# Packed expert weights, one column read per tile, three weight loads per group and 48 matmuls at three starts, in a two-layer attention and expert kernel

## The reference, cut to what matters

```python
x = x + L0_attention(layernorm(x), ctx)             # 16 heads, rotary
x = x + L0_ffn(layernorm(x), gate_w, w13, w2)       # 64 experts, 8 per token, inner width 128
x = x + L1_attention(layernorm(x), ctx)             # over the 256 features: softmax(q^T k) v
x = x + L1_ffn(layernorm(x), router_w, ...)         # 16 experts, 4 per token, inner width 224
```

## Time and profile before

| | us |
|---|---|
| median of 3 runs | 764.34 (762.84 to 764.79) |
| the profiled execution | 764.58 |
| its span, first to last instruction | 762.8 |
| PE busy | 506.1 (66%) |
| PE weight loads | 377.7 (50%) |
| DVE busy | 378.6 (50%) |
| ACT busy | 224.9 (29%) |
| GpSimd (POOL) busy | 351.0 (46%) |
| DMA | 162.57 MB, mean 213 GB/s |

### The profile page before, as it was taken

One profiled execution on the slowest core, in us unless ns is written; L12 is line 12 of the kernel. 1 busy time (PEld: TensorE's weight loads), 2 busy tenths in 40 slices (PEclk: granted clock), 3 DMA queues, 4 the chain that ended last, 5 costly groups with the idle time before them and its releaser, 6 DMA issues.

```text
span 762.8 us, 12322 instructions
## 1 busy us (share of the span) xinstructions
PE 506.1 (66%) x3519; PEld 377.7 (50%) x3519; DVE 378.6 (50%) x1235; ACT 224.9 (29%) x578; POOL 351.0 (46%) x476
## 2 busy tenths in 40 slices
PE   1725986878867323998879951677618878777760
PEld 1611543434432113977668840555517767666750
DVE  8955555877773530443334425888522222222226
ACT  0550353555555101332223311344302111211210
POOL 9483111445544550554455460144465545455530
PEclk9975888998996655999999975677859999999995
DMA  5199997644665796799974328611247767787837
GB/s 166 45 191 309 310 279 212 176 153 135 204 206 184 256 416 191 235 341 323 302 263 165 92 93 306 270 56 63 78 145 227 247 225 252 227 249 248 282 128 275
DMA packets 88291, 162.57 MB, mean 213 GB/s; under 512 B 13742, under 2 KB 58814, under 8 KB 86448
## 3 DMA queue, kind: packets, MB, share of 16 engines
q1 hardware_dynamic: 62208, 104.83, 43.1%
q0 software_dynamic: 13968, 32.29, 11.6%
q10 hardware_dynamic: 12064, 24.84, 11.1%
HBM read 103.56 MB, written 66.78 MB: 223 GB/s over the span
## 4 chain that ended last, share of the span: by engine, by line
PE 17%; DMA 14%; issue 12%; SPq 8%; DVE 5%; POOL 1%; another core or an unknown queue 1%; POOLq 1%; ACT 1%; DVEq 1%
DMA hd_side<-held 5%; PE hd_ps_up L1216 5%; DMA listed<-sc_empty,sc_index 2%; DMA sc_tile_rows<-listed 2%; PE hd_ps_out L1222 2%; DMA rows<-hd_side_out,hd_side_target 2%; SPq L426 2%; SPq L424 2%; DMA sc_rows<-rows 2%; PE sc_ps L1697 2%; PE hd_ps_x L1194 1%; PE sc_ps L1759 1%; SPq L1604 1%; PE sc_ps L1709 1%
## 5 line engine op out<-in xcount | busy, mean ns | idle before, releaser
L990 DVE TENSOR_REDUCE at_top<-at_ps_top 128x2 f32<-128x512 f32 x128 | 83.3, 683 | 59.6 <-PE at_ps_top L901 54.3
L1363 POOL DMA_INDIRECT rows<-hd_out,hd_rows x64 | 62.4, 975 | 72.9 <-DVE hd_out L1314 45.9
L1062 ACT ACTIVATE at_prob<-at_ps_score 128x512 f32<-128x512 f32 x128 | 72.3, 594 | 53.7 <-PE at_ps_score L919 42.4
L1759 PEld LDWEIGHTS sc_ps<-sc_t_turned,e_up_w 128*112 128x112 f32 x672 | 82.2, 183 | 5.7 <-issue 3.0
L1216 PE MATMUL hd_ps_up<-hd_x_turned,e_arena 128*128 128x160 f32 x512 | 84.9, 310 | 0.0
L1759 PE MATMUL sc_ps<-sc_t_turned,e_up_w 128*112 128x128 f32 x672 | 83.6, 279 | 1.9 <-DMA e_down_w<-in_down 1.8
L1216 PEld LDWEIGHTS hd_ps_up<-hd_x_turned,e_arena 128*128 128x128 f32 x512 | 78.3, 197 | 8.9 <-issue 6.2
L685 POOL DMA_INDIRECT held<-e_extended,e_address x64 | 63.1, 986 | 33.7 <-issue 18.9
L901 PE MATMUL at_ps_top<-e_arena 96*128 96x256 bf16 x256 | 58.0, 316 | 25.2 <-PEq L107 21.3
L1660 POOL DMA_INDIRECT rows<-sc_out,sc_target x42 | 41.3, 982 | 67.9 <-DVE sc_out L1903 61.7
L1351 DVE TENSOR_TENSOR hd_inner<-hd_silu,hd_ps_up 128x160 f32<-128x160 f32 x64 | 20.6, 321 | 92.1 <-ACT hd_silu L1301 62.0
(11 more groups left out here) (266 smaller groups left out, 930.5 us busy)
## 6 DMA issues: line engine op xcount, KB each, us to landing
e_arena<-in_weights SPq DMA_DIRECT2D x52, 384.0 KB
e_up_w<-in_up SPq DMA_DIRECT2D x42, 448.0 KB
held<-e_empty ACTq DMA_DIRECT2D x16, 960.0 KB, 5.7
hd_rows<-held SPq DMA_DIRECT2D x15, 768.0 KB
e_down_w<-in_down SPq DMA_DIRECT2D x42, 224.0 KB
sc_rows<-rows SPq DMA_DIRECT2D x8, 1024.0 KB, 13.7
sc_tile_rows<-listed SPq DMA_DIRECT2D x42, 144.0 KB
parts<-op_parts SPq DMA_DIRECT2D x8, 576.0 KB
```

The costliest lines, as they stand in the source:

```text
L990: nc.vector.reduce_max(top[:, 2 * h:2 * h + 2], ps_top[at % TOPS][:], AX_X).then_inc(top_found, 1)
L1062: nc.scalar.activation(prob[at % RING][:], ps_score[at % SCORES][:], ACT.Exp, scale=scale).then_inc(prob_ready, 1)
L1363: nc.gpsimd.indirect_dma_start(rows_out, to, out_ap, None, bounds_check=TOKENS * LAYER0.chosen - 1, oob_is_err=False).then_inc(semaphore, 16)
L1759: op = nc.tensor.matmul(ps_up[u % 2][:, part, c * P:(c + 1) * P], up_w[u][:, k, at:at + W], t_turned[u % 2][:, k, :], start=k == 0, stop=k ...
```

## The change

- The second experts' up and down weights become one array in DRAM, per expert 128 rows of 896 + 512 numbers (the last 16 rows of the down part are zeros), and one SBUF buffer per set with two views. SP loads them in one transfer of 704 KiB. The array has entries of zeros behind the 16 experts.
- SP reads the column once per tile and shifts it right by 3 to get the entry of the weights; `tile_expert` is no longer read by SP. For the first six tiles the six reads stand ahead of the first load.
- PE waits for 16 per tile on the weights' semaphore in place of 32.
- DVE picks weight and target before it waits for silu, with a new wait for the tile's rows.
- In the first experts SP loads 3 weights after each of groups 0 to 9 and 2 after group 10, in place of 4 after each of groups 0 to 7.
- 48 matmuls on constants stand at the start of PE's program of the first experts, after `first_layer_done` in the second phase, and ahead of the second experts' first turn (after the plan is known).

```diff
-WARM_UP = 24
+WARM_UP, START_WARM = 24, 48
...
-        self.up = [s.sbuf(f"up_w{u}", [P, 2, 2 * layer.inter], F32) for u in U]
-        self.down = [s.sbuf(f"down_w{u}", [layer.width, layer.chunks, D], F32) for u in U]
-        self.transfers = [(self.up, up_dram), (self.down, down_dram)]
+        down_at = 4 * layer.inter
+        self.w = [s.sbuf(f"w{u}", [P, down_at + layer.chunks * D], F32) for u in U]
+        self.up = [w[:, 0:down_at].rearrange("p (k n) -> p k n", k=2) for w in self.w]
+        self.down = [w[0:layer.width, down_at:].rearrange("p (c n) -> p c n", c=layer.chunks) for w in self.w]
+        self.weights_dram = weights_dram
...
-    def load(self, sp, i, u):
-
+    def column(self, engine, i, u):
         at = bass.ds(i * self.layer.unroll + u, 1)
-        e = sp.value_load(self.tile_expert[0:1, at], min_val=0, max_val=self.layer.experts - 1)
-        for to, of in self.transfers:
-            sp.dma_start(to[u][:], of[bass.ds(e, 1)].rearrange("a p k n -> (a p) k n")).then_inc(self.loaded[u], 16)
...
+        return engine.value_load(self.tile_column[0:1, at], min_val=0, max_val=self.layer.columns + 2 * self.layer.unroll - 1)
+
+    def load(self, sp, column, u):
+
+        e = column >> (self.layer.lists.bit_length() - 1)
+        sp.dma_start(self.w[u][:], self.weights_dram[bass.ds(e, 1)].rearrange("a p n -> (a p) n")).then_inc(self.loaded[u], 16)
...
-    E, RING, OUTS, INNERS, BEFORE = LAYER0.experts, 4, 8, 8, 56
+    E, RING, OUTS, INNERS, BEFORE, AGAIN = LAYER0.experts, 4, 8, 8, 56, 3
...
-                for e in range(EACH * g, EACH * (g + 1)):
-                    if e + ring.SLOTS < E:
-                        ring.load(sp, e + ring.SLOTS)
+                for e in range(ring.SLOTS + AGAIN * g, min(ring.SLOTS + AGAIN * (g + 1), E)):
+                    ring.load(sp, e)
...
+            for _ in range(START_WARM):
+                nc.tensor.matmul(ps_b[:, 0, 0:P], consts.earlier[:], consts.ones[:], start=True, stop=True)
             turn_side(0)
...
             last = groups(sp)
+            columns = [experts.column(sp, 0, u) for u in range(U)]
             for u in range(2):
-                experts.load(sp, 0, u)
+                experts.load(sp, columns[u], u)
             sp.wait_ge(experts.scattered, 16 * layer.chosen * B)
             for u in range(U):
-                load_tile(0, u)
+                load_tile(0, u, columns[u])
             sp.wait_ge(tile_loaded[1], 16)
             for u in range(2, U):
-                experts.load(sp, 0, u)
+                experts.load(sp, columns[u], u)
             with sp.Fori(1, last + 1) as i:
                 for u in range(U):
+                    c = experts.column(sp, i, u)
                     sp.wait_ge(inner_ready, i * U + u - U + 1)
                     sp.sem_inc(sp_parted, 1)
-                    load_tile(i, u)
+                    load_tile(i, u, c)
                     sp.wait_ge(down_done, i * U + u - U + 1)
                     sp.sem_inc(sp_parted, 1)
-                    experts.load(sp, i, u)
+                    experts.load(sp, c, u)
...
             pe.wait_ge(joined.first_layer_done, 1)
+            keep_warm(START_WARM)
...
-                pe.wait_ge(weights_loaded[u], (i + 1) * (16 * len(experts.transfers)))
+                pe.wait_ge(weights_loaded[u], i * 16 + 16)
...
+            keep_warm(START_WARM)
             turn(0, 0)
...
+                dve.wait_ge(tile_loaded[u], i * 16 + 16)
...
+                pick(i, u, free)
                 dve.wait_ge(silu_done, i * U + u + 1)
-                pick(i, u, free)
```

More of the change, by code:

```diff
@@ L401, with __init__ @@
 class Experts:
-    def __init__(self, s, layer, up_dram, down_dram):
+    def __init__(self, s, layer, weights_dram):
         self.layer = layer
@@ L1602, in _, with load_tile @@
         def _(sp):
-            def load_tile(i, u):
-                c = sp.value_load(experts.tile_column[0:1, bass.ds(i * U + u, 1)], min_val=0, max_val=layer.columns + 2 * U - 1)
+            def load_tile(i, u, c):
                 sp.wait_ge(cleared[u], i * 16 + 16)
@@ L1711, in attend, with keep_warm @@
                 op.then_inc(attended, 1)
-            def keep_warm():
-                for _ in range(WARM_UP):
+            def keep_warm(count=WARM_UP):
+                for _ in range(count):
                     nc.tensor.matmul(ps_t[0][:, 0, :], consts.earlier[:], consts.ones[:], start=True, stop=True)
             pe.wait_ge(joined.first_layer_done, 1)
+            keep_warm(START_WARM)
             for t in STEPS:
@@ L1927, in two_layers @@
                merge_biases, gate0, weights0,
-               gate1, gate1_bias, up1, down1, out):
+               gate1, gate1_bias, weights1, out):
     def scratch(name, shape, dtype=F32):
@@ L1955, in two_layers @@
         with ExitStack() as expert_stack:
-            experts = Experts(Space(nc, expert_stack, "e1_", joined), LAYER1, up1, down1)
+            experts = Experts(Space(nc, expert_stack, "e1_", joined), LAYER1, weights1)
             second_inputs = SecondInputs(Space(nc, expert_stack, "f_", joined), ctx, ctx_turned, gate1, gate1_bias)
@@ L1989, in gates @@
         return w.T.reshape(2, P, -1).transpose(1, 0, 2)
+    E1, W1, UP1 = LAYER1.experts, LAYER1.width, 4 * LAYER1.inter
+    past = (LAYER1.columns + 2 * LAYER1.unroll - 1) // LAYER1.lists + 2
+    weights1 = np.zeros((past, P, UP1 + LAYER1.chunks * D), np.float32)
     up1 = np.concatenate([L1_ffn_gate_proj, L1_ffn_up_proj], axis=2)
+    weights1[0:E1, :, 0:UP1] = up1.reshape(E1, 2, P, -1).transpose(0, 2, 1, 3).reshape(E1, P, UP1)
+    weights1[0:E1, 0:W1, UP1:] = L1_ffn_down_proj.reshape(E1, LAYER1.chunks, W1, D).transpose(0, 2, 1, 3).reshape(E1, W1, -1)
     return {
@@ L2007, in laid_out @@
         "gate1_bias": np.broadcast_to(L1_ffn_expert_bias, (P, LAYER1.experts)),
-        "up1": by_contraction(up1),
-        "down1": L1_ffn_down_proj.reshape(LAYER1.experts, LAYER1.chunks, LAYER1.width, D).transpose(0, 2, 1, 3),
+        "weights1": weights1,
     }
```

## The result

The changed kernel takes **744.0 us** (median of 4 runs, 736.71 to 746.47); the kernel before, run beside it, 764.57 (762.84 to 766.94). The ratio is 0.970, interval 0.966 to 0.975. In a second series of runs it was 0.976 (0.966 to 0.985). The forecast was 733.5 us, range 716 to 752: the direction is right, two thirds of the gain came.

A forecast was written before the change was run, and what follows sets the result against it. It took SP's program to pace the second experts and a full DMA to hold up the first. 764.6 less 19.6 + 3.5 + 0 + 6.5 + 1.5 = 31.1 gives 733.5 us, range 716 to 752.

The forecast's parts named there:

- Part 4: First experts: three weight loads per group instead of four move 3.1 MB from full DMA; gain 6.5 us, bound 9.3.
- Part 1: Second experts: one load and one register read fewer per tile on SP; 4.01 to 3.45 us a tile, 19.6 us.
- The HBM side: Second experts: by the skill's 358 GB/s, 1.03 MB need 2.9 us a tile; the gain would lie nearer to 32.
- Part 2: Second experts' first six tiles: 20.0 us before, 13.5 of PE work at full clock; gain 3.5 us, bounds 0 and 5.
- Part 3: Second experts: DVE picks weight and target before waiting for silu; 0 us by itself, bounds 0 and 1.9.
- Part 5: 48 matmuls at three starts: 1.5 us in the first experts, 0 ahead of features, second experts' gain counted in Part 2.
- DMA takes over: Second experts: transfers don't get closer than at present, pace 3.75 us a tile; 744 us in all; chance 0.18.
- Only put off: First experts: moved weights only delay rows of groups 12 to 15, nothing of 6.5 us remains; 740 us; chance 0.12.
- The lost warm-up: Expert stages' starts: clock back at half when the first tile comes, 1.5 and 1.5 us go; 736.5 us; chance 0.05.
- Everything meshes: Second experts at pace 3.1, 9 us gained in the first experts, 5 in Part 2; 716.5 us; chance 0.11.
- The late packed load: Second experts: 704 KiB loads land late, at 18.4 us the pace is 4.6, 20.6 us lost; 777 us; chance 0.04.

The follow-up runs named there:

- no_clears: The changed kernel without GpSimd's clears in the second experts' loop, the list emptied once before the features: loop 99.2 us, total 759.52 against 771.26 before.
- packed_only: The kernel before with only the packed weights and the one column read per tile: ratio 0.988 (0.979 to 0.998), loop 129.7 us.
- after_no_warm: The changed kernel without the three groups of 48 matmuls: ratio 0.969 (0.965 to 0.973), loop 126.4 us.
- ring_only: The kernel before with only three weight loads per group in place of four in the first experts: ratio 0.993 (0.990 to 0.997).
- fewer_bytes: The changed kernel loading only 224 of 704 KiB of weights per tile in the second experts' loop: ratio 0.970 (0.966 to 0.975), loop 125.2 us.
- three_deep: The changed kernel with the turned rows' copy moved from ACT to DVE and the second experts' tiles three deep, not two: ratio 0.981, loop 127.5 us.

## Why the prediction was right, and where it was off

Its total was 10.5 us too low: 733.5 against 744.0. In the two profiles 20.8 us went, of 31.1 forecast. The mechanism was right in the two large parts, and the amounts were off in both directions: part 4 gave more than its bound and made up for others, so some of the nearness is luck.

- **Part 1** (19.6, pace 3.45): 15.2 came, pace 3.57. Right: SP was the bound, it now waits for PE, and PE's wait for rows is gone; DMA's share rose to 0.84, not over 0.9. Wrong was the step that left SP's 0.68 us steps as unexplained and set the floor by PE, DMA and GpSimd's busy time. GpSimd's 2.1 us a tile were counted as a third engine with room to spare; what its clears do to the others wasn't. No_clears shows that both the slow steps and the late signals hang on them. The floor of 3.1 was too high as well: in no_clears the three parts take 1.75, 0.22 and 0.86 us where 1.84, 0.28 and 0.87 were read, 2.83 in all, and DMA moves the 0.97 MB that a tile then needs beside that.
- **The HBM side.** no_clears moves 342 GB/s at a share of 0.97 of the engines. The Trainium skill (DMA: Bandwidth & Descriptors, Where 436 GB/s comes from) has the HBM side hold such traffic at about 358 GB/s. This stretch stays under it, but the kernel before moves 412 GB/s over the 21 us from 265 to 286, weights in and rows out. The measurement decides: the figure isn't a limit for both directions together, and the 2.9 us a tile that the prediction worked out from it is no floor that these runs show.
- **Part 2** (3.5): the six tiles gave 4.9, but the first tile's rows came 3.6 later, 1.3 in all; by the second profiles 2.9 and 2.4, 0.5 in all. That the reads ahead and two loads of 704 KiB would stand directly before the rows in the queue was seen as time inside a wait; it wasn't.
- **Part 3** (0): it "helps 3.45 to be reachable" is as much as the runs bear; between packed_only and the changed kernel lie 3 to 6 us of loop (3.3 to after_no_warm), near the scatter.
- **Part 4** (6.5, bound 9.3): 10.6 came, 10.8 in ring_only alone, more than the bound. The bound was 3.1 MB at 337 GB/s; PE's own side, 14.4, was the one that held. Waits inside the stage fell by 6.7 us, and PE's busy time from the first turn to the end by 5.5 (138.40 to 132.94), as less of the work ran at the lower clock behind a wait: the granted clock over it rises from 0.93 to 0.96.
- **Part 5** (1.5, features 0): the clock rose in the first experts, the features got nothing, both as forecast, but the 1.5 us don't reach the end, within 0.4%. The 48 matmuls took 4.3 to 4.4 us where 5.2 was estimated. At the second experts the clock was lost again in the 6.31 us before the first tile, so the gain that was put into part 2 for it did not come.
- **Other stages**: attention and features were 6.5 us longer in this profile after. That is scatter as far as the runs tell: the attention takes 227.3 to 233.2 us over all the profiles, the features 107.5 and 113.4 before and 108.9 and 110.3 after. It is over half of the miss against the profile's own time, so the parts themselves gave 27 of the 31.1.

On part 1 the trace of the kernel before had a hint: the slow steps of the earlier trace rows, from 636.44 on, stand beside a run of GpSimd's, which its busy share doesn't show.

```profile
636.45 0.97 POOL L1655 DMA_INDIRECT listed<-sc_empty,sc_index  x1 [0.30 <-issue]
...
637.78 0.98 POOL L1660 DMA_INDIRECT rows<-sc_out,sc_target  x1 [0.16 <-issue]
639.07 0.98 POOL L1655 DMA_INDIRECT listed<-sc_empty,sc_index  x1 [0.30 <-issue]
```

The rivals: "DMA takes over" gave 744 us, the number that came, by luck: fewer_bytes refutes it as a cause. "Only put off" is refuted by ring_only. The lost warm-up came true at the second experts, and cost nothing that the runs can show. "Everything meshes" did not come; no_clears shows what stood in its way. The late packed load showed itself at one place only, the first tile.

## What to carry to other kernels

An engine with busy share to spare can still be what paces the others: test it by taking its work away, not by its share. When instructions on unrelated engines are slow or late at the same instants, look for one that is busy in a row at those instants. And where small loads stand in one queue with large ones, look at how far behind the large ones the first small load of a stage is asked for: 6.2 us behind the last of them in place of 0.75 brought it 3 to 4 us sooner, though the end didn't show it.

## What the runs showed of the hardware that was not expected

While GpSimd issues indirect transfers in a row (0.98 and 0.97 us each, 0.16 to 0.30 between them), engines that wait for PE start 5.4 us after PE's records end (up to 6.0 in three_deep), several at once, as five of PE's signals, whose records end 2.3 to 5.4 us earlier, come within 0.3 us; and SP's program takes 0.7 us for steps that take 0.3. Without the clears the late signals are gone, and one of SP's slow steps is left. In the chain of waits of the changed kernel this is a piece under no engine's name:

```profile
617.58 0.38 ACT sc_t_turned L1821
617.96 7.69 another core or an unknown queue
625.64 0.02 issue
625.67 0.39 ACT sc_silu L1827
```

The Trainium skill (Perfetto Trace Analysis, Per-instruction lifecycle: what the profiler-reported window actually captures) says that the profiled interval of such a transfer on GpSimd is the writing of its descriptors and not the movement; no run here separates the two, and nothing in it says that others are held up meanwhile. Whether it is the writing, the transfers' small packets or the spacing that matters stays open: one clear and one scatter per 2.6 us do it, one scatter per 2.83 us doesn't, and nothing in between was run.
